# Pair levels as 32x32 products, value columns in a new order, scans ahead of the pair weights

## The reference, cut to what matters

```python
Lam = softplus(Lp * dl)                    # dl = x @ Wdl.T, [B, T, H, LV]
cg = cumsum(g, axis=1)                     # g from dt = softplus(x @ Wdt.T + dt_bias)
decay = exp(where(tri, cg[t] - cg[s], NEG))
levels[t, s] = 0 if s == t else floor(log2(s xor t)) + 1
lam_ts = Lam[t, h, levels[t, s]]
Wmat = (Q K^T * S**-0.5) * decay * lam_ts
Y = Wmat @ V
o = Y @ Wout.T + x
out = layernorm(o) * ln_g + ln_b           # the "second norm"
```

## Time and profile before

| | us |
|---|---|
| three runs: median (lowest to highest) | 1076.66 (1075.57 to 1076.85) |
| profiled execution: time | 1077.35 |
| profiled execution: span | 1075.7 |
| PE busy | 1028.9 (96%) |
| DVE busy | 890.4 (83%) |
| ACT busy | 693.4 (64%) |
| POOL busy | 247.9 (23%) |

### The profile page before, as it was taken

The page is one execution under the profiler, slowest core; times in us unless marked ns, Lnnn a source line. Parts: engine busy times, 40 slices in busy tenths (PEclk is TensorE's granted clock), DMA queues, the critical chain, the costliest instruction groups (busy, mean ns, idle before and its releaser), DMA issues. The chain is left out here.

```text
span 1075.7 us, 18976 instructions
## 1 busy us (share of the span) xinstructions
PE 1028.9 (96%) x6188; PEld 667.0 (62%) x6188; DVE 890.4 (83%) x2038; ACT 693.4 (64%) x1509; POOL 247.9 (23%) x235
## 2 busy tenths in 40 slices
PE   7999999999999999999999999999999999999985
PEld 3666657566665766657566665766657566565763
DVE  5897897979889797987979889797987979889776
ACT  4693857749386592957749385683947649385682
POOL 0040310313122031311303131031311203131186
PEclk9999999999999999999999999999999999999998
DMA  4000000000000000000000000000000000000535
GB/s 150 21 1 10 2 20 11 0 29 0 19 10 19 10 0 29 0 19 10 0 29 0 26 4 19 10 0 29 0 19 10 10 20 0 29 0 19 175 108 157
DMA packets 31907, 27.61 MB, mean 26 GB/s; under 512 B 1552, under 2 KB 25744, under 8 KB 31760
## 3 DMA queue, kind: packets, MB, share of 16 engines
q1 hardware_dynamic: 31888, 27.37, 7.9%
HBM read 15.57 MB, written 11.80 MB: 25 GB/s over the span
## 5 line engine op out<-in xcount | busy, mean ns | idle before, releaser
L1765 POOL TENSOR_TENSOR pair<-pair,cgt 128x512 f32<-128x512 f32 x64 | 88.9, 1417 | 505.1 <-DVE pair L1527 505.1
L992 ACT ACTIVATE gx<-p 128x512 f32<-128x512 f32 x256 | 145.8, 596 | 25.8 <-PE p L546 21.3
L544 PE MATMUL p<-x1Th,Gl 128*128 128x512 f32 x256 | 119.9, 468 | 0.3 <-ACT gx L992 0.3
L947 ACT ACTIVATE gelu<-p,bias_u 128x512 f32<-128x512 f32 x32 | 22.0, 687 | 141.9 <-PE p L491 141.9
L546 PE MATMUL p<-x1Th,Gh 128*128 128x512 f32 x256 | 100.8, 394 | 0.0
L545 PE MATMUL p<-x1Tl,Gh 128*128 128x512 f32 x256 | 100.2, 392 | 0.0
L655 PEld LDWEIGHTS p<-vbd,pair 128*128 128x128 f32 x512 | 62.0, 191 | 40.4 <-issue 26.8
L1795 POOL TENSOR_TENSOR skip<-skip,W 128x512 f32<-128x512 f32 x15 | 19.2, 1281 | 275.1 <-DVE skip L1310 275.1
L604 PE MATMUL p<-rs,GT 128*128 128x120 f32 x512 | 65.3, 281 | 15.9 <-ACT rs L1063 11.9
L604 PEld LDWEIGHTS p<-rs,GT 128*128 128x128 f32 x512 | 59.6, 191 | 31.8 <-ACT rs L1063 24.8
L655 PE MATMUL p<-vbd,pair 128*128 128x128 f32 x512 | 73.3, 286 | 0.0
(11 more groups left out here) (270 smaller groups left out, 2657.9 us busy)
## 6 DMA issues: line engine op xcount, KB each, us to landing
xin<-in_x SPq DMA_DIRECT2D x16, 256.0 KB, 2.7
hx_scratch<-vdw SPq DMA_DIRECT2D x15, 256.0 KB, 2.6
res_scratch<-res SPq DMA_DIRECT2D x14, 256.0 KB, 2.1
gx<-in_weights SPq DMA_DIRECT2D x1, 1216.0 KB, 9.9
vp<-hx_scratch SPq DMA_DIRECT2D x4, 256.0 KB, 3.5
GT<-res_scratch SPq DMA_DIRECT2D x4, 256.0 KB, 3.1
out<-vp SPq DMA_DIRECT2D x4, 256.0 KB, 3.4
W<-in_weights SPq DMA_DIRECT2D x1, 746.0 KB, 11.1
```

The lines of the kernel that those rows point to most:

```text
L544: pe.matmul(head_bank(h)[:, :], tile(Gl, h), x1Th[:, :], start=True, stop=False)
L992: act.activation(tile(gx, h, T), head_bank(h)[:, :], ACT.Copy).then_inc(R["gx_copied"], 1)
L1765: pool.tensor_tensor(pw, pw, spread(cgt[:, H * n:H * n + H].unsqueeze(2), [128, H, CHUNK]), ALU.subtract)\
```

## The change

1. **Order of the value columns.** Once, in `later_weights`, DVE reorders the columns of `Wvdw` in four more instructions: values, dt, output projection, then the four high levels (level by head), then the six low levels (head by level). All views of `vdw` and `lam` follow. The store of the output projection reads other columns of the same size.
2. **Low levels from tokens in chunk order.** ACT makes a second copy of the turned input, `x1P`, in which tile c holds chunk c of all four token tiles. `values` is now two products per tile: 336 columns from `x1T` and 96 columns from `x1P`.
3. **Pair levels as 32x32 products.** `nodesT` now has in its partitions 32n to 32n + 31 what belongs to token tile n. `pair_levels(i, half)` multiplies the 32x32 diagonal block n of `left` with those rows for each c: 8 products with 32 rows, 32 columns and 512 streamed columns for tiles 0 and 1 (banks 2 and 0), later 8 for tiles 2 and 3. The second half stands inside `node_matrices` and waits for DVE's reading of the first two banks.
4. **Node matrices** use banks 4, 3, 4, 3; groups 2 and 3 wait for ACT's copies of groups 0 and 1.
5. **DVE's order.** `level_weights` and `stats2` stood ahead of `node_lams`. Now `node_lams`, `node_rows`, both scans, then `pair_lams(0)`, `pair_weights(0)`, `pair_lams(1)`, `stats2`, `pair_lams(2)`, `pair_lams(3)`, the rest of the scan, `top1`, `level_weights`. `pair_weights` is only the product with the scores.
6. **ACT's order.** Two of the `pair_distance` instructions go ahead of the last two head copies; the copies of `left_halves` stand between the `pair_decay` instructions; `rstd2` stands behind them, directly ahead of `own_values`.
7. **The last batch**: the same, with `cell_out` behind `node_rows`, `level_weights` behind the four level products, and two of the `end_add` behind `own_heads(3)` and `tile_sum(3)`. SP's load of one stored batch waits for `level_weights`.

```diff
 def values(j):   # PE
-    pe.matmul(P1[(2 + n) % 5][:, 0:VDW], tile(x1T, n), w("Wvdw"), start=True, stop=True)\
+    bank = P1[(2 + n) % 5]
+    pe.matmul(bank[:, 0:336], tile(x1T, n), w("Wvdw", 0, 336), start=True, stop=True)
+    if n == 0:
+        pe.wait_ge(R["x1P_ready"], j + 1)
+    pe.matmul(bank[:, 336:VDW], tile(x1P, n), w("Wvdw", 336, VDW), start=True, stop=True)\
         .then_inc(R["vdw_ps"], 1)
...
 def node_matrices(i):   # PE
     for g in range(4):
-        if g == 3:
-            pe.wait_ge(R["m_copied"], 4 * i + 1)
-        bank = P1[(4, 0, 3, 4)[g]]
+        if g == 2:
+            pair_levels(i, 1)
+        if g >= 2:
+            pe.wait_ge(R["m_copied"], 4 * i + g - 1)
+        bank = P1[(4, 3)[g % 2]]
...
-def pair_levels(i, n):
-    if n == 0:
+def pair_levels(i, half):
+    pe.wait_ge(R["ident_loaded"], 16)
+    if half == 0:
         pe.wait_ge(R["lev_abs"], i + 1)
+        pe.wait_ge(R["r_copied"], 4 * i + 2)
         pe.wait_ge(R["nodesT_ready"], i + 1)
     else:
-        pe.wait_ge(R["dlam_ready"], 4 * i + n)
-    pe.matmul(P1[2][:, :], k("left"), tile(nodesT, n, 512), start=True, stop=True).then_inc(R["lam_ps"], 1)
+        pe.wait_ge(R["dlam_ready"], 4 * i + 2)
+    for c in range(4):
+        for n in (2 * half, 2 * half + 1):
+            rows, cols = slice(32 * n, 32 * n + 32), slice(32 * c, 32 * c + 32)
+            mm = pe.matmul(P1[(2, 0)[n % 2]][cols, :], k("left")[rows, rows], tile(nodesT, c, 512)[rows, :],
+                           start=True, stop=True)
+    mm.then_inc(R["lam_ps"], 1)
...
 # ACT, stages
+                    pair_distance(i, 0, 2)
                     heads(i, 14, H)
+                    pair_distance(i, 2, TILES)
+                    pair_decay(i, 0, 2)
+                    left_halves(i, 0, 3)
+                    pair_decay(i, 2, 3)
+                    left_halves(i, 3, TILES)
+                    pair_decay(i, 3, TILES)
                     if later(i):
                         rstd2(i - 1)
-                    pair_distance(i)
-                    left_halves(i, 0, 2)
-                    pair_decay(i)
-                    left_halves(i, 2, TILES)
                     own_values(i)
                     node_matrices(i)
...
                     turned1(j)
+                    chunk_order(j)
                     high_part(j)
...
 # DVE, stages
                 if i is not None:
-                    level_weights(i)
-                    if later(i):
-                        stats2(i - 1)
                     node_lams(i)
                     node_rows(i)
                 if j is not None:
                     scan_inputs(j)
-                if i is not None:
-                    pair_weights(i, 0)
-                if j is not None:
                     scans(j)
-                if j is not None:
+                if i is not None:
+                    pair_lams(i, 0)
+                    pair_weights(i, 0)
+                    pair_lams(i, 1)
+                    if later(i):
+                        stats2(i - 1)
+                    pair_lams(i, 2)
+                    pair_lams(i, 3)
+                if j is not None:
+                    scan_outs(j)
                     top1(j)
+                if i is not None:
+                    level_weights(i)
...
 # DVE, last
-                level_weights(i)
                 dve.wait_ge(R["c_ready"], B)
                 node_lams(i)
+                node_rows(i)
                 cell_out()
-                node_rows(i)
+                pair_lams(i, 0)
                 pair_weights(i, 0)
+                for n in range(1, TILES):
+                    pair_lams(i, n)
+                level_weights(i)
                 own_heads(i, 0)
```

More of the change, by code:

```diff
@@ L154, in build @@
         x1T = sb("x1T", T)
+        x1P = sb("x1P", T)
         VDW = 432
@@ L965, in turned1, with chunk_order @@
                 act.activation(x1T[:, :], P1[0][:, :], ACT.Copy).then_inc(R["x1T_ready"], 1)
+            def chunk_order(i):
+                if later(i):
+                    act.wait_ge(R["vdw_ps"], 4 * i)
+                act.wait_ge(R["x1T_ps"], i + 1)
+                act.activation(view(x1P[:, :], "p (c k t) -> p c k t", c=4, k=TILES),
+                               view(P1[0][:, :], "p (k c t) -> p c k t", k=TILES, c=4), ACT.Copy).then_inc(R["x1P_ready"], 1)
             def high_part(i):
@@ L1041, in level_decay, with pair_distance, pair_decay @@
                 act.activation(e4[:, 128:320], lev[:, 64:256], ACT.Exp, scale=-1.0).then_inc(R["e4_ready"], 1)
-            def pair_distance(i):
-                for n in range(TILES):
+            def pair_distance(i, a, b):
+                for n in range(a, b):
                     act.wait_ge(R["diff_ready"], 4 * i + n + 1)
                     act.activation(tile(pair, n, 512), tile(pair, n, 512), ACT.Abs).then_inc(R["diff_abs"], 1)
-            def pair_decay(i):
-                for n in range(TILES):
+            def pair_decay(i, a, b):
+                for n in range(a, b):
                     act.wait_ge(R["diff_abs"], 4 * i + n + 1)
@@ L1285, in first @@
                 scans(0)
+                scan_outs(0)
                 gate0(0, 0)
@@ L1515, in level_weights @@
                 for n, at in enumerate((0, 128)):
-                    dve.scalar_tensor_tensor(tile(alpha, n, 64), e4[:, at:at + 64], k("alpha_mask", TILES * n, TILES * n + 1),
-                                             l[:, 6 + n], ALU.mult, ALU.mult)
-                dve.tensor_tensor(view(alpha[:, 128:256], "p (l m) -> p l m", l=2),
-                                  view(e4[:, 192:320], "p (l m) -> p l m", l=2), l[:, 8:10], ALU.mult)\
-                    .then_inc(R["alpha_steps"], 1)
+                    dve.scalar_tensor_tensor(rows(tile(alpha, n, 64), 1)[:, 0], rows(e4[:, at:at + 64], 1)[:, 0],
+                                             k("alpha_mask", TILES * n, TILES * n + 1), high[:, n], ALU.mult, ALU.mult)
+                for n in (2, 3):
+                    last = dve.tensor_tensor(rows(tile(alpha, n, 64), 1)[:, 0], rows(e4[:, 64 * n + 64:64 * n + 128], 1)[:, 0],
+                                             high[:, n], ALU.mult)
+                last.then_inc(R["alpha_steps"], 1)
             def token_rows(i):
@@ L1528, in token_rows, with pair_lams @@
                     .then_inc(R["cgrow_ready"], 1)
+            def pair_lams(i, n):
+                dve.wait_ge(R["decay_ready"], 4 * i + n + 1)
+                dve.wait_ge(R["lam_ps"], 2 * i + n // 2 + 1)
+                dve.tensor_tensor(tile(pair, n, 512), tile(pair, n, 512), P1[(2, 0)[n % 2]][:, :], ALU.mult)\
+                    .then_inc(R["dlam_ready"], 1)
             def pair_weights(i, n):
-                dve.wait_ge(R["decay_ready"], 4 * i + n + 1)
-                dve.wait_ge(R["lam_ps"], 4 * i + n + 1)
-                dve.tensor_tensor(tile(pair, n, 512), tile(pair, n, 512), P1[2][:, :], ALU.mult)\
-                    .then_inc(R["dlam_ready"], 1)
                 dve.wait_ge(R["s_ps"], 4 * i + n + 1)
@@ L1641, in stages @@
                     scan_inputs(j)
+                    scans(j)
                 if i is not None:
+                    pair_lams(i, 0)
                     pair_weights(i, 0)
+                    pair_lams(i, 1)
+                    if later(i):
+                        stats2(i - 1)
+                    pair_lams(i, 2)
+                    pair_lams(i, 3)
                 if j is not None:
-                    scans(j)
-                if j is not None:
+                    scan_outs(j)
                     top1(j)
+                if i is not None:
+                    level_weights(i)
                 if i is not None:
@@ L1735, in last @@
                 level_sum(i, 3)
+                own_heads(i, 3)
                 end_add(POOL_ADDS + 2)
-                end_add(POOL_ADDS + 3)
-                own_heads(i, 3)
-                end_add(POOL_ADDS + 4)
                 tile_sum(i, 3)
-                for b in range(POOL_ADDS + 5, B):
+                for b in range(POOL_ADDS + 3, B):
                     end_add(b)
```

72 lines of the change are left out of this document (43 added, 29 removed).

## The result

| | before | after |
|---|---|---|
| median (lowest to highest), us | 1076.71 (1075.57 to 1076.85) | 1135.53 (1133.86 to 1137.15) |
| profiled execution: span, us | 1075.7 | 1134.4 |
| mean granted clock | 0.995 | 0.953 |
| one turn of the loop, us | 64.2 | 68.25 |

The ratio is 1.0549, with a 95% interval of 1.053 to 1.0567. Forecast were 1103 and a range of 1083 to 1124: the direction was right, the size was less than half of what came, and the time lies outside the range.

The account below looks back on a forecast made before the run. PE was taken as the bound, working 62.91 of 64.24 us a turn. Fourteen turns at +1.85 (+25.9), set-up +0.9, turn i = 0 -2.05 and last batch +1.0 make +25.8 on 1077.35: 1103 us, range 1083 to 1124.

Parts of the forecast that it names:

- sums ready: In a loop turn, DVE's sums for the second norm (`stats2`) end at 527.6.
- PE idle for it: In the node matrices, PE stands 3.9 us for ACT's first copy, to 531.4; before it stood 0.26.
- from there to `levels(3)`: From `own_heads(0)`, DVE's stretch shrinks from 14.12 to 12.28 us; PE's `levels(3)` starts at 548.0, +1.6 us.
- Groups 2 and 3 take 0.89 + 1.08: PE's time for the last two node-matrix groups behind its wait for ACT's copy, in us.
- the scores 0.99: PE's time for the scores, behind the last node-matrix groups and ahead of the values and own heads, in us.
- this case as a rival: Clock falls too: PE work after the wait takes up to 4.0 us longer a turn; 1117, or 1131 in all; chance 0.22.
- the window 1060 to 1065: Profile window of the kernel before, PE working 1.61 of 5 us at clock 1.00, cited against the clock falling.
- Sums sooner: `node_lams` takes 2.86 us even beside POOL, sums 2.3 us earlier, a turn -0.45 us, total 1071; chance 0.16.
- The wait does not bind: Each turn goes like i = 0, -2.05 us, needing the sums by 524; total 1048; chance 0.07.
- Set-up: Four more DVE instructions on the way to the first `x1`: 0 to 1.2 us, taken as +0.9.
- Last batch: POOL's additions and the stores behind them set the end; POOL starts about 1.2 us later; taken as +1.0.
- Values: On PE, four further products of 96 columns and 96 fewer in four others: 0 to +0.4 us, taken as +0.25.

Follow-up runs that it names:

- experiment 3: The kernel after, with twelve filling products whose results are overwritten put on PE ahead of its wait for ACT's first node-matrix copy: 1107.7 us, ratio 1.0301.
- experiment 6: The kernel of experiment 3 with four filling products in place of twelve: 1123.1 us, ratio 1.0441.
- Experiment 5: The kernel after, with GpSimd's level values cut to one head of sixteen from the first loop turn on, so results differ: 1124.1 us, ratio 1.0439.
- Experiments 1 and 2: The kernel after, with ACT's second norm behind its node-matrix copies (1) or DVE's sums for it ahead of the node products (2): 1064.7 and 1067.3 us.
- experiment 10: The kernel of experiment 1 with three filling products on PE ahead of the first turning of x1 in the set-up: 1064.4 us, ratio 0.9894.
- Experiment 9: The kernel of experiment 1 with DVE's order in the last batch as in the kernel before: 1062.7 us, ratio 0.9872.
- experiment 7: The kernel of experiment 1 with DVE's second level product ahead of the score product and the second norm behind the last level sum: 1137.4 us, ratio 1.0566.
- 4: The kernel before, with only the second norm's part changed: DVE's sums behind the scans, ACT waiting for them ahead of own values: 1180.5 us, ratio 1.0967.

## Why the prediction failed

**Step by step, one turn.** The turn of the kernel after lies 24.4 us behind that of the forecast (`node_lams` at 537.58 and at 513.18); with that taken off:

| step | forecast | measured |
|---|---|---|
| group of eight small products, start to next start | 1.0 | 1.02 |
| `node_lams` | 5.2 | 4.96 |
| sums ready | 527.6 | 527.7 |
| ACT idle ahead of the second norm | 3.6 | 3.84 |
| first copy of node matrices done | 531.3 | 531.4 |
| PE idle for it | 3.9 | 3.77 |
| `own_heads(0)` | 535.65 | **537.93** |
| from there to `levels(3)` | 12.35 | 12.38 |
| turn | 66.1 | **68.25** |

Up to the end of the wait no step is off by more than 0.3 us. The copy behind `node_lams` (0.66 and not 0.22) was not foreseen to grow, which made up for the products. The one step of the turn that failed is what PE needs behind the wait, "Groups 2 and 3 take 0.89 + 1.08" and "the scores 0.99": these durations were taken from rows at clock 1.00, and behind the wait the clock was half. That is 2.3 us at the own heads, 2.2 us in the turn by experiment 3, and 28 of the 33 us by which the total was missed; the set-up has 2.7 more and the last batch 0.9.

**The choice was mine, not the profile's.** The forecast knew this case as a rival, at 0.22, with 1131 if it struck in every turn. Experiment 3 ends at 1107.7, so the forecast of 1103 was nearly that of the wait alone; and 1131 for both together fell 4 us short of 1135.5. I held the window 1060 to 1065 against it: clock 1.00 with PE working in 1.61 of 5 us. But a mean over 5 us doesn't tell how long PE stood at a stretch, nor what the clock did next: the very next window has 0.56. The trace of the kernel before shows both:

```profile
1063.65 0.43 PE L663 MATMUL p<-ym,K 128*32 128x128 f32 x8 [2.90 <-DVE ym L1560]
```

PE stood 2.90 us there and twice more for 0.49 and 0.69 us, and from 1066 on the clock is at 0.50. And the sentence "here PE is fully busy on both sides of the wait" was no reason, since the work ahead doesn't carry the clock through: in the kernel after PE works in 1.71 of the 2 us ahead of the gap, and the clock falls all the same. The Trainium skill (TensorE: Matmul & The Clock Gate, Part 1) has an idle stretch put the clock to half; by that rule this rival should have been the forecast. The runs agree for the loop's gaps of 3.35, 3.77, 5.3 to 5.6 and 5.4 us, which brought the clock down in every turn; of the gap of 2.78 us in experiment 6 they say "in ten turns of fourteen", which "an idle stretch" alone doesn't tell. Last, the range was cut inside the rival (at 1124 of 1110 to 1131), with the case "in all turns" beyond its end, though the text had no reason for "half of the turns", so "in all" should have been inside it. (Turns alike in their gap can differ in their clock, as experiment 6 showed later; with the gap of the kernel after none did.)

**Sums sooner** (0.16, 1071). Its premise holds (2.87 us without POOL's work beside it) and its price does not. That "all that hangs on the sums is 2.3 us earlier" overlooks what the same text says, that the bank is ready at 523.4 when DVE comes at 524.3: 0.9 us of slack, and no more can be gained. Experiment 5 has 0.8. With PE's gap at 3.35 us instead of 3.8 that run came to 1124, 11 us below the kernel after and not below the kernel before.

**The wait does not bind** (0.07, 1048). Experiments 1 and 2 take the wait away and come to 1065 and 1067. The turn for i = 0 changed by -2.0, as forecast, but it has no `stats2`, and 1.26 us of DVE's path are missing in it. With it a turn gains 1.1 (63.17), so 1048 was too low by 14 us for that alone.

**Set-up.** The copy `x1P` at nothing and "+0.9" for the reordering stood against +3.6. PE's stop of 1.45 us there, 0.81 before, ends with the clock at half again, and with products put behind it the clock stays up (experiment 10); the values take 1.55 us a tile at half and not 0.8. The same term as in the loop, in a place where I had not looked for it.

**Last batch.** The start of POOL's additions is the right bound; it came 1.6 us late (16.43 against 14.82 behind the pair differences), forecast 1.2, since the node products took 5.24 us there and not 4.05, and the batch ended 1.9 late, forecast 1.0. Experiment 9 gives it back.

**Values.** PE's work in a turn without the gap fell by 1.15 (61.76), forecast 1.5 - 0.25 = 1.25. Right.

## What to carry to other kernels

A small instruction that waits costs what is queued behind it: ask of each one that moves who makes what it waits for, when that is ready in the new order, and what stands behind it on its own engine. A gap that this opens on TensorE is paid twice, once in waiting and once in the work behind it at half clock; cost the steps behind a gap at both levels, and compare its length with those that a trace shows. Here 3.35 us and more brought the clock down in every turn of four kernels, 2.78 us in ten of fourteen, so "it falls in every turn" would have been the first guess for 3.9. When an edit's engine time falls (here 1.2 us of TensorE work a turn) and the kernel gets slower, look for such a wait before giving up the edit: moving it made this change a gain of 1.1%, and 1.9% with the rest.

## What the runs showed of the hardware

- The clock's fall depends on more than the length of the gap. In one kernel, with the same work ahead and the same gap of 2.78 us, it fell in ten turns of fourteen and stayed in four (experiment 6). With 1.06 us it never fell in the loop (3); with 3.35, 3.77, 5.3 to 5.6 and 5.40 us it fell in all fourteen turns (5, the kernel after, 7, 4). In the set-up a stop of 1.45 us ends with the clock down (the kernel after), and one of 1.88 us with the clock up (10).
- The loss comes behind the gap. In the turn of experiment 7 shown above the clock is 1.00 until the last 0.1 us of an idle stretch of 5.3 us, and 0.54 in the 2 us from 513 on; in the kernel after it falls in the middle of the gap and is back to 1.00 only some 4.7 us after PE has begun to work again.
- Beside GpSimd's additions, VectorE's products of 128 x 64 elements take about 1.2 us each (2.51 for two, against 0.47 for two with GpSimd idle), five times as long. That GpSimd's work is the cause is shown by experiment 5 for the node products (2.87 us for five without it, 4.96 beside it). The Trainium skill (SBUF — State Buffer, "SBUF: two separate sides") says that a VectorE instruction with two SBUF inputs and a GpSimd one that reads SBUF hold a shared port in turn, each for its whole length; the 1.2 us are about one of GpSimd's additions (2.52 for two), as that rule would have it.
